# Who adds the second table's mask to a tile's row numbers: VectorE instead of GpSimd

## What is computed

```
gate = xn @ Wg + bg;  idx = top_k(gate, 2);  mask = one_hot(idx, 8).sum(-2)
h = gelu(einsum('td,edh->teh', xn, W1) + b1);  y = einsum('teh,ehd->ted', h, W2) + b2
out = x + einsum('ted,te->td', y, mask)
```

## Time and profile before

| | |
|---|---|
| the profiled execution's time | 758.38 us |
| its span | 756.7 us |
| median of three runs | 759.71 us |
| PE busy | 689.9 us (91%) |
| DVE busy | 599.9 us (79%), 1301 instructions |
| POOL busy | 583.8 us (77%), 685 instructions |
| ACT busy | 502.8 us (66%) |
| stores, L1477 | 91, 92.7 us busy, 67.7 us idle ahead of them |

### The profile page before, as it was taken

How to read it: one execution, slowest core, us unless ns; L and a number is a source line. 1 busy time by engine, 2 the same in 40 slices (tenths; PEclk the granted TensorE clock), 3 DMA queues, 4 the chain that set the end, 5 groups by cost and what they waited for, 6 DMA issues and landing times.

```text
span 756.7 us, 17027 instructions
## 1 busy us (share of the span) xinstructions
PE 689.9 (91%) x5408; PEld 357.1 (47%) x5408; DVE 599.9 (79%) x1301; ACT 502.8 (66%) x1017; POOL 583.8 (77%) x685
## 2 busy tenths in 40 slices
PE   5888999999999999999999999998899999999930
PEld 2322233333333333333333333232798999999830
DVE  3788989999999999999999999998977555554410
ACT  4755577786777877777777776665865666666610
POOL 7649596988989889898898988989777755555553
PEclk9998999999999999999999999999999999999975
DMA  7630010011010111101110001051513523233300
GB/s 269 184 107 29 0 30 15 15 43 43 29 45 15 43 43 30 43 15 43 43 29 29 20 26 43 15 141 37 142 52 109 144 79 90 75 91 89 94 13 0
DMA packets 47958, 45.42 MB, mean 60 GB/s; under 512 B 6981, under 2 KB 42576, under 8 KB 47872
## 3 DMA queue, kind: packets, MB, share of 16 engines
q1 hardware_dynamic: 41888, 31.60, 14.7%
q0 software_dynamic: 5984, 12.74, 4.8%
HBM read 27.73 MB, written 18.34 MB: 61 GB/s over the span
## 4 chain that ended last, share of the span: by engine, by line
PE 67%; DVE 14%; issue 8%; ACT 5%; POOL 3%; DVEq 1%; SPq 0%; DMA 0%; POOLq 0%; ACTq 0%
PE scores_ps L453 16%; PE ctx_ps L465 11%; PE z_ps L472 9%; PE scores_ps L622 9%; DVE e L978 9%; PE ctx_ps L648 4%; PE z_ps L648 4%; ACT x_rows L764 3%; PE job_ps L492 2%; PE job_ps L501 2%; PE job_ps L528 2%; PE job_ps L557 2%; POOL out L1477 1%; PE job_ps L513 1%; PE job_ps L484 1%
## 5 line engine op out<-in xcount | busy, mean ns | idle before, releaser
L759 ACT ACTIVATE e<-e 128x2048 f32<-128x2048 f32 x128 | 245.1, 1914 | 145.0 <-DVE e L978 145.0
L978 DVE SCALAR_TENSOR_TENSOR e<-scores_ps,bound_mem 128x2048 f32<-128x2048 f32 x128 | 293.2, 2291 | 33.5 <-PE scores_ps L453 28.6
L1477 POOL DMA_INDIRECT out<-e,near x91 | 92.7, 1018 | 67.7 <-POOL near L1470 32.5
L857 ACT ACTIVATE e<-scores_ps,bound_mem 128x128 f32<-128x128 f32 x364 | 104.0, 372 | 53.0 <-PE scores_ps L622 52.4
L1450 POOL TENSOR_TENSOR ctx_part<-ctx_part,z_inv 128x1024 f32<-128x1024 f32 x60 | 115.8, 1930 | 23.8 <-DVE z_inv L994 23.8
L472 PE MATMUL z_ps<-e,one_column 128*32 128x512 f32 x1024 | 133.4, 592 | 0.0
L1462 POOL TENSOR_TENSOR ctx_sum<-ctx_sum,ctx_part 128x512 f32<-128x512 f32 x90 | 115.4, 1282 | 7.8
L622 PE MATMUL scores_ps<-e,bound_mem 128*128 128x128 f32 x728 | 97.5, 277 | 4.9 <-DVE bound_mem L1174 3.3
L622 PEld LDWEIGHTS scores_ps<-e,bound_mem 128*128 128x128 f32 x728 | 88.5, 192 | 7.8 <-issue 4.4
L986 DVE STREAM_TRANSPOSE ctx_part<-ctx_ps 128x512 f32<-128x512 f32 x128 | 90.3, 705 | 1.8 <-PE ctx_ps L465 1.8
L1424 POOL DMA_INDIRECT sorted_rows<-x_rows,slot x64 | 64.4, 1006 | 18.1 <-issue 16.9
(11 more groups left out here) (182 smaller groups left out, 1001.2 us busy)
## 6 DMA issues: line engine op xcount, KB each, us to landing
near<-sorted_rows SPq DMA_DIRECT2D x91, 130.0 KB, 2.2
near<-in_x SPq DMA_DIRECT2D x16, 256.0 KB, 2.9
bound_mem<-in_adjT SPq DMA_DIRECT2D x4, 1024.0 KB, 9.1
x_post<-in_x SPq DMA_DIRECT2D x16, 256.0 KB, 2.8
sorted_rows<-pad_row SPq DMA_DIRECT2D x1, 3640.0 KB, 15.8
out<-e,near POOLq DMA_INDIRECT x91, 2.7
sorted_rows<-x_rows,slot POOLq DMA_INDIRECT x64, 2.6
bound_mem<-in_w SPq DMA_DIRECT2D x1, 1024.0 KB, 5.6
```

The lines of the kernel that those rows point to most:

```text
L759: nc.scalar.activation(every, every, ACT.Exp, scale=SCORE_SCALE).then_inc(exp_done, 1)
L857: nc.scalar.activation(e_flat[:, h_at:h_at + P], scores_ps[:, i % 2, k * P:(k + 1) * P], ACT.Gelu, bias=part_flat[:, bias_at:bias_at + 1]) ...
L978: dve.scalar_tensor_tensor(out=e[:, s % E_RING], in0=scores_ps[:], scalar=-CLIP, in1=to, op0=ALU.max, op1=ALU.min).then_inc(clipped, 1)
L1477: nc.gpsimd.indirect_dma_start(out=out_rows, out_offset=bass.IndirectOffsetOnAxis(ap=near_u[:, id_at:id_at + 1], axis=0), in_=e_flat[:, at ...
```

## The change

`mask_id` moves from GpSimd's program to VectorE's. The sum is the same, element by element. On GpSimd it stood just ahead of the tile's store; on VectorE the mask of tile k - 2 stands in slot k, behind that tile's `add_bias` and ahead of its `finish`. The store's own waits stay as they are.

```diff
--- before.py
+++ after.py
@@ -1183,6 +1183,14 @@
                 dve.tensor_tensor(part_flat[:, at:at + D], near[:, x2_at:x2_at + D],
                                   b2_pair[:, bass.ds(offsets_of[i][2], D)], ALU.add).then_inc(x2b_ready, 1)
 
+            def mask_id(i):
+                r, of = i % XT_RING, i - MASKED_AT
+                if of == 0:
+                    dve.wait_ge(mask_ready, 1)
+                dve.wait_ge(xt_loaded[r], 16 * (i // XT_RING + 1))
+                id_u = near_u[:, xt_at[r] + ID_AT:xt_at[r] + ID_AT + 1]
+                dve.tensor_tensor(id_u, id_u, mask[:, of:of + 1], ALU.add).then_inc(id_masked, 1)
+
             def finish(i):
                 dve.wait_ge(y_ready, i + 1)
                 dve.wait_ge(x2b_ready, i + 1)
@@ -1306,6 +1314,8 @@
                     count_tiles(1)
                 if k >= 2:
                     add_bias(k - 2)
+                if MASKED_AT <= k - 2:
+                    mask_id(k - 2)
                 if k == 0:
                     scale_last(0)
                     scale_last(2)
@@ -1461,14 +1471,6 @@
                     first = to
                 nc.gpsimd.tensor_tensor(to, first, ctx_part[:, at], ALU.add).then_inc(ctx_added, 1)
 
-            def mask_id(i):
-                r, of = i % XT_RING, i - MASKED_AT
-                if of == 0:
-                    pool.wait_ge(mask_ready, 1)
-                pool.wait_ge(xt_loaded[r], 16 * (i // XT_RING + 1))
-                id_u = near_u[:, xt_at[r] + ID_AT:xt_at[r] + ID_AT + 1]
-                nc.gpsimd.tensor_tensor(id_u, id_u, mask[:, of:of + 1], ALU.add).then_inc(id_masked, 1)
-
             def store(i):
                 pool.wait_ge(o_ready, i + 1)
                 need(pool, id_masked, i - MASKED_AT + 1)
@@ -1540,8 +1542,6 @@
                 if k == 13:
                     scatter(14, (2, 3))
                 while stored < stored_by(k):
-                    if MASKED_AT <= stored:
-                        mask_id(stored)
                     store(stored)
                     stored += 1
                 if k == 0:
```

## The result

The changed kernel takes 735.93 us (median of 4 runs, 733.91 to 736.71), beside it the kernel before 760.14 (757.6 to 761.69): a ratio of 0.9681, 95% interval 0.9647 to 0.9714, so some 24 us less. A second timing with more runs gave 0.9662 (0.9640 to 0.9685) and 733.84 us. Forecast were 733.5 us, in a range of 729 to 741. The profiled run after took 735.62 us with a span of 733.9.

The account below looks back on a forecast made before the run. GpSimd's masked stores, 2.143 us per tile against TensorE's 1.896, were taken to bound the end. Starting the last store 25.49 us earlier gave a 731.21 us span, 732.9 or 734.2 of time; forecast 733.5, range 729 to 741.

Parts of the forecast that it names:

- GpSimd's spacing: Stores from tile 21: 1.29 us apart while behind, instead of 2.143 per tile; caught up after 11 tiles, then 1.896.
- TensorE's lost time: Tiles 71 to 90: with no load late, the last finish comes at 720.87 instead of 724.76 us, 3.89 earlier.
- The last store: Tile 90's store: no queue ahead of it, so it starts at 722.01 instead of 747.50 us, 25.49 earlier.
- the wake of 0.85 us: Time from a finish's end on VectorE to its store's start on GpSimd, taken as 0.85 us; other end 0.58 less.
- the sum: Whole kernel: span of 756.70 less 25.49 gives 731.21 us; with 1.68 beyond the span, 732.9 us of time.
- The end behind the last store: From the last store's start to the span's end: 9.20 us kept, because the same DMA ends it.
- The rival of a drain that shrinks with the backlog: GpSimd's drain at the program's end: up to 6.5 us less, 727 us; chance 7%.
- The room for it: VectorE's idle time ahead of each finish, 0.40 us per tile, taken to hide a mask of 0.14 us.
- That a late finish does no harm: VectorE's finishes: 0.1 us late costs nothing but at the last tile, since following work has margins of some 1 us.
- The engines blocking each other: Rival: stores and VectorE's bias additions and masks exclude each other, 0.67 us per tile, 39 us more, 772 us; chance 3%.
- The level: Starting time: 732.9 us by the profiled run, 734.2 by the median, 1.33 higher; 733.5 chosen between the two.

Follow-up runs that it names:

- e2: Kernel before, masks kept on GpSimd but each issued ahead of the store two tiles earlier: 733.97 us, ratio 0.9677.
- e3: Changed kernel with every second mask back on GpSimd just ahead of its store: 734.63 us, ratio 0.9672.
- e10: Changed kernel with GpSimd waiting, behind its last store, for that store's landing before it drains: 734.88 us, ratio 0.9666.
- e9: Changed kernel with one small memset (128x8) on GpSimd behind its last store: 733.54 us, ratio 0.9664.
- e6: Changed kernel with three more 128x128 additions on VectorE behind each of the 70 masks: 734.22 us, ratio 0.9644.
- e7: Changed kernel without the stores of the last six tiles: 723.27 us, ratio 0.9519.

## Why the prediction was right

**GpSimd's spacing.** Stores of 1.29 us while behind, caught up after 11 tiles, 1.896 us from there: measured 1.3 us (601.44 to 615.75 in 11 steps), the first waiting store is tile 33's, and VectorE's finishes of tiles 21 to 88 lie (720.60 - 593.58) / 67 = 1.896 us apart. The reason given, a queue that cannot prepare the store while it waits for the mask ahead of it, is what e2 tests, and it held: the order of GpSimd's own instructions alone brings the gain. e3 adds that it is a threshold and no sum of shares.

**TensorE's lost time.** From tile 21's finish to tile 90's were forecast 720.87 - 591.11 = 129.76 us and measured 723.35 - 593.58 = 129.77. The gaps from 684 us on the earlier trace rows are gone: TensorE is busy for all of 640 to 684 and until its last product.

**The last store.** Of the wake of 0.85 us, 0.8 were measured behind each finish (721.68 behind 720.60 + 0.29, 723.47 behind 722.38 + 0.29). But the last store came 1.12 us behind its finish's end. The sum missed that tile 90's finish follows tile 89's by only 0.97 us while stores cannot follow closer than 1.29: 723.47 + 1.29 = 724.76. This term was 0.27 us too small. Measured from tile 21's finish on, the gain is 25.27 us, the sum had 25.49.

**The end behind the last store.** 9.20 us were kept, 9.14 came (724.76 to 733.90). The number was right, and in all of these traces whose GpSimd ends with the same store the drain is over 7.9 us behind it. The reason given, that the same DMA ends the program, is not what the runs show: in e10 the drain begins once that DMA has landed and still takes 7.9 us, and in e9 it is over 7.9 us behind a memset. The rival of a drain that shrinks with the backlog had 7%; nothing of it showed.

**VectorE.** The mask took 0.15 us (0.14 was taken) and was hidden, as forecast. The room for it was mis-sized, on the safe side: e6 shows at least 0.6 us where I had read 0.4 from the idle time. That a late finish does no harm, which the prediction had argued, is shown there too: 0.2 us late cost TensorE nothing.

**The engines blocking each other.** This rival, by which the kernel would have become slower, did not come about. In the changed kernel stores take 0.98 us and bias additions 0.29 us beside them (the store at 617.41 covers the one at 617.53), and the mask at 617.74 takes its 0.15 us under the same store. The nearest thing to it is in e6, where the three additions (652.46 to 653.15) run under a store and it takes 1.08 us instead of 0.98 (from 620 to 726 us the mean is 1.06 against 0.98). By the rule of the Trainium skill ("SBUF — State Buffer", section "SBUF: two separate sides") a VectorE instruction with two SBUF inputs and a GpSimd instruction that reads SBUF exclude each other for the whole of an instruction. The traces here show no such thing: the 0.1 us is a sixth of the three additions' time. Whether a store counts as reading SBUF in the sense of that rule, no run here shows.

**The level.** The sum started from a profiled run that took 1.33 us less than the median. The median of 735.93 lies 2.4 us above 733.5, and 733.84 in the second timing; that is the spread from run to run; in the profiled executions it lies ahead of tile 21 (the table above). Against the profiled run's own 735.62 us the sum, 732.9, is 2.7 us short: 2.47 of them lie ahead of tile 21's finish, 0.27 at the last store.

## What to carry to other kernels

On GpSimd an operation recorded with 0.2 us cost 0.8 because the indirect DMA right behind it waited for its result, and the queue then prepared nothing ahead: read the cost from the starts of what stands around it, and move the producer some instructions ahead before moving it to another engine. Look for an engine that is a little slower per step than the one that seems to bound the stage; as long as there are buffers the loss shows nowhere, and then all of it stands at the end. Idle time ahead of an instruction was only a lower bound of VectorE's room: the instruction could come a little late, and the "issue" time shrank under added work. When runs spread by more than the effect, count from an instruction ahead of which the programs are the same.

## What the runs showed of the hardware that I had not expected

- VectorE ran the 32-bit addition on 128x1 as CUSTOM_DVE_ANT_0 on 128x2 uint16, in 0.146 to 0.158 us.
- GpSimd's drain at the end of the program is over 7.9 us behind GpSimd's last work (7.4 in e7); begun later, when the last DMA had landed, it still took 7.9 us (e10). Where it was over early (e7), the program ended 0.5 us behind the start of VectorE's last instruction.
- On GpSimd a small operation between two indirect DMAs that the next one doesn't wait for adds some 0.1 us (1.38 against 1.29 us from store to store), one that the next DMA waits for adds 0.79.
- VectorE could be kept busy for 37.45 us of a stage of 44 (85%), with no marked wait ahead of the finishes, and TensorE lost nothing (e6).
